# Moving dispatch operations, a dummy matmul and fourteen relus in a recurrent kernel with routed experts

## What is computed

```python
def step(carry, inp):
    h_ssm = silu(h_ssm @ A.T + bxt)
    y_ssm = h_ssm @ Cw.T + Cb + dxt
    hh = h_rnn @ W_hh.T + b_hh
    r = sigmoid(i_r + h_r)
    z = sigmoid(i_z + h_z)
    n = tanh(i_n + r * h_n)
    h_rnn = (1.0 - z) * n + z * h_rnn
    y_rnn = h_rnn @ proj_w.T + proj_b
    fused = gxt[:, :1] * y_ssm + gxt[:, 1:2] * y_rnn
...
h = layernorm(x) * (1 + ca) + sa
x = x + ga * attn(h)                       # 8 x 512 x 128
h = layernorm(x) * (1 + cb) + sb
x = x + gb * ffn(h)    # expert argmax(softmax(h @ gate_w.T)), relu(h @ w1[e] + b1[e]) @ w2[e] + b2[e], times its probability
```

## Time and profile before

| what | value |
|---|---|
| median of 3 runs | 695.22 us (694.72 to 696.77) |
| profiled execution, its own time | 694.69 us |
| its span | 692.8 us |
| PE busy | 673.0 us (97%) |
| DVE busy | 523.5 us (76%) |
| ACT busy | 423.8 us (61%) |
| POOL busy | 119.6 us (17%) |
| chain that ended last | PE 96%, issue 1%, DVE 1%, DMA 1% |

### The profile page before, as it was taken

How to read it: one execution, slowest core, us unless ns; L and a number is a source line. 1 busy time by engine, 2 the same in 40 slices (tenths; PEclk the granted TensorE clock), 3 DMA queues, 4 the chain that set the end, 5 groups by cost and what they waited for, 6 DMA issues and landing times.

```text
span 692.8 us, 35329 instructions
## 1 busy us (share of the span) xinstructions
PE 673.0 (97%) x13692; PEld 632.1 (91%) x13692; DVE 523.5 (76%) x3189; ACT 423.8 (61%) x2677; POOL 119.6 (17%) x211
## 2 busy tenths in 40 slices
PE   8999999999999999999999999999999999999991
PEld 5899999989999999999999999999999999998891
DVE  4777777777887777887888788888887888876463
ACT  4555555556666666567666775676667656766540
POOL 4011111111011111112112211111212212211122
PEclk9999999999999999999999999999999999999996
DMA  8916000603522100044322000552210006434262
GB/s 307 363 64 224 8 7 7 226 31 129 189 97 85 53 15 15 14 164 176 131 81 78 19 18 19 201 178 95 94 61 23 21 19 242 148 111 137 70 228 57
DMA packets 46152, 72.79 MB, mean 105 GB/s; under 512 B 6236, under 2 KB 28834, under 8 KB 45858
## 3 DMA queue, kind: packets, MB, share of 16 engines
q1 hardware_dynamic: 41922, 65.11, 26.8%
q0 software_dynamic: 2048, 4.20, 2.1%
q10 hardware_dynamic: 2016, 1.25, 0.6%
HBM read 14.44 MB, written 21.17 MB: 51 GB/s over the span
## 4 chain that ended last, share of the span: by engine, by line
PE 96%; issue 1%; DVE 1%; DMA 1%; ACT 0%; POOL 0%; POOLq 0%
PE rs_bank L1183 34%; PE nz_bank L1183 23%; PE hid_bank_b L1183 12%; PE work L1183 11%; PE y_bank L1183 9%; PE hid_bank_a L1183 7%; DMA yg<-rows,pos 0%; POOL yg L694 0%; DMA rows<-y_sb 0%; POOLq L498 0%; DVE fin_g L1168 0%; ACT hid_b L775 0%; DVE y_sb L1162 0%; DVE u L1100 0%; ACT xT L772 0%
## 5 line engine op out<-in xcount | busy, mean ns | idle before, releaser
L1183 PE MATMUL nz_bank<-h_ring,wg 128*64 128x16 f32 x4088 | 207.1, 211 | 0.0
L787 ACT ACTIVATE r_fac<-rs_bank 128x8 f32<-128x8 f32 x512 | 91.3, 178 | 170.7 <-PE rs_bank L1183 163.3
L1183 PE MATMUL rs_bank<-s_ring,ws_sb 128*64 128x128 f32 x1024 | 195.1, 272 | 0.0
L1183 PEld LDWEIGHTS nz_bank<-h_ring,wg 128*64 128x64 f32 x4088 | 160.6, 136 | 1.2
L1183 PE MATMUL rs_bank<-mw,wg 128*64 128x8 f32 x2044 | 146.4, 202 | 0.1
L1183 PE MATMUL rs_bank<-u,wg 128*64 128x8 f32 x2044 | 140.0, 206 | 0.2
L1092 DVE TENSOR_TENSOR_SCAN nz_bank<-r_fac,nz_bank 128x16 f32<-128x16 f32 x512 | 99.2, 194 | 48.4 <-ACT r_fac L787 30.8
L1183 PEld LDWEIGHTS rs_bank<-s_ring,ws_sb 128*64 128x64 f32 x1024 | 127.2, 136 | 9.3
L1096 DVE SCALAR_TENSOR_TENSOR mw<-v_fac,h_ring 128x8 f32<-128x8 f32 x512 | 85.7, 167 | 57.6
L1183 PEld LDWEIGHTS rs_bank<-mw,wg 128*64 128x64 f32 x2044 | 102.9, 135 | 19.1 <-DVE mw L1096 4.6
L793 ACT ACTIVATE v_fac<-nz_bank 128x8 f32<-128x8 f32 x512 | 90.7, 177 | 42.1
(11 more groups left out here) (162 smaller groups left out, 1077.0 us busy)
## 6 DMA issues: line engine op xcount, KB each, us to landing
wx<-w_all SPq DMA_DIRECT2D x59, 578.0 KB, 3.5
rows<-zeros SPq DMA_DIRECT2D x3, 4096.0 KB, 14.6
rows<-y_sb SPq DMA_DIRECT2D x67, 64.0 KB, 1.6
w_all<-in_w SPq DMA_DIRECT2D x2, 2048.0 KB, 15.3
xs_sb<-rows SPq DMA_DIRECT2D x55, 64.0 KB, 3.3
x_sb<-in_x SPq DMA_DIRECT2D x1, 1920.0 KB, 8.0
out<-o_sb SPq DMA_DIRECT2D x19, 64.0 KB, 2.5
out<-o_sb ACTq DMA_DIRECT2D x13, 64.0 KB, 2.0
```

Of the source, the lines that this page charges most:

```text
L787: nc.scalar.activation(r_fac[:, k, :, 1], r_cols(q, t), ACT.Tanh, scale=0.5).then_inc(rn_ready, 1)
L1183: last = nc.tensor.matmul(out[c:c + COLS], weights[:, c:c + COLS], moving, start=start, stop=stop, skip_group_check=skip_group_check)
```

## The change

There are four edits.

1. For the first four groups the ten dispatch operations no longer stand in steps 2 to 11, one in each, but in steps 6, 6, 9, 10, 10, 10, 11, 11, 12, 12. `rows_at`, from which SP's loads are written, is one step later.
2. In step 9 of a tile the dummy product of a step with room stands ahead of the transpose of h2 and not behind it.
3. The entry for step 9 is gone from `DVE_EARLY`. The units of every step stay the same; seven second relus (tiles 8, 9, 13, 15, 16, 20, 22, step 9) are ACT's where they were DVE's.
4. In the tail a second relu goes to ACT only before step (NT+1)*T = 528; seven relus of slots 51 to 54 are DVE's where they were ACT's.

```diff
-DVE_EARLY = {2: 15, 4: 15, 9: 23, 10: 23}
+DVE_EARLY = {2: 15, 4: 15, 10: 23}
...
+LAY_OUT = (6, 6, 9, 10, 10, 10, 11, 11, 12, 12)
+
+
 def dispatch_at(k, n):
 
     at = (last_tile(k) + 2) * T
-    return at + (2 + n if at < NT * T else 12 + n // 2)
+    return at + (LAY_OUT[n] if at < NT * T else 12 + n // 2)
...
-            if k < NG - 1 and what[0] in "AC" and what[2]:
+            if k < NG - 1 and u < (NT + 1) * T and what[0] in "AC" and what[2]:
                 on_act.add(what)
...
                     unit(kind, n, second)
-                if w == 9:
-                    tile_work(c, q, w, g)
                 if exists(c):
                     room = 0 if g in RELU_OPEN else ROOM - taken(g) - len(units)
                     if room == 2:
                         hold_clock(g, len(units), 2 * P)
                     if room == 1:
                         hold_clock(g, len(units), P)
+                if w == 9:
+                    tile_work(c, q, w, g)
+                if exists(c):
                     if g == 0:
```

## The result

| | before | changed |
|---|---|---|
| median | 694.97 us (693.74 to 696.77, 6 runs) | 698.24 us (698.02 to 699.07, 6 runs) |
| ratio | | 1.0047, 95% interval 1.0031 to 1.0064 |
| profiled execution, its span | 694.69, 692.8 | 698.25, 696.3 |
| last h_ring write of the recurrence | 632.48 us | 636.21 us |
| from there to the end of the span | 60.28 us | 60.11 us |

The changed kernel is slower by 3.3 us, and the place is the recurrence: its last step ends 3.73 us later, while the tail is 0.17 shorter. The page shows how little a mean can tell here. Its busy shares are those of before to within a point (PE 97%, DVE 75%, ACT 61%), and the granted clock is 0.992 again. Only the chain of waits has moved: PE has 93% of it instead of 96%, VectorE and ScalarE one point more each.

A forecast was written before the change was run, and what follows sets the result against it. Each step is bounded by a loop through three engines with 0.57 us free before the scan. Move +3.35, loads +0.25, dummy -0.5, relus +0.1, tail -0.15 give +3.05 on 695.22: 698.2 us, range 696.8 to 699.8.

The forecast's parts named there:

- What sets the end: Every recurrence step: work before the scan is free up to 0.57 us after h_ring; any excess lengthens the step equally.
- step 10, four tiles: Tiles 7, 14, 21, 28: passed, expert_f, ended in a chain make the scan 0.57 us late, 2.28 in all.
- step 11: Same four tiles: first_f then block_f make the scan 0.29 us late, 1.16 in all.
- step 12: Same four tiles: place then expert behind onehot, scan 0.12 us late, 0.48 in all, 1.1 at the upper end.
- step 6: Same four tiles: over then n_slots, scan 0.14 us late in tiles 7 and 14, 0.33 in 21 and 28; 0.94.
- removed, steps 2 to 7: Dispatch operations leaving their old steps, such as ended from step 7, give back about 1.5 us.
- The loads: SP's first-slot loads come 1.27 us later against their use; tile 21's group waits, +0.25 us (0 to 1.1).
- Rival B: First rows land late in all four groups: +1.1 us in place of +0.25, 699.1 to 702 us; chance 0.09.
- The dummy: Dummy ahead of h2's transpose: ten steps of 1.25 to 1.28 us after step 9 fall to 1.21, -0.5 us.
- rival C: Long single steps in tiles 6, 4 and 28 vanish, some 1.05 us; 693.7 with A; chance 0.04 including the unseen.
- The relus and the tail: Seven step-9 relus moved to ScalarE cost +0.1 us; seven tail relus moved to VectorE free xT copies, -0.15 us.
- Rival A: Dependent dispatch operations cost no more than independent ones, so the move nets 0.1 us: 694.8 us; chance 0.15.

The follow-up runs named there:

- the last two layouts: Dispatch steps chosen for each group, with edits 2 and 4 and fewer waits: 695.38 us; the same with a first slot's rows loaded before its weights: 693.26 us.
- the kernel with fewer waits: Changed kernel in which ended waits only for passed and expert only for expert_f: 698.74 us, 1.0027 of the kernel before.
- the first four kernels of the experiments' table: Only the new layout 700.70 us; changed without the new layout 696.16; changed with fewer waits 698.74; a layout for each group 695.38.
- the last three: Changed with all ten dispatch operations in step 10: 710.48 us; per-group layout with rows loaded before weights: 693.26; changed kernel again: 698.57.

## Why the prediction was right

The forecast was 698.2 us; the measured median is 698.24. It was right by its mechanism. That the two agree to 0.04 is luck: the forecast stood on a median of 695.22 for the kernel before, which is 694.97 with six runs. The change was put at +3.05 and measured at +3.27, with 2.2 to 4.4 as its interval, and the terms of the sum that came out too small or on the wrong group nearly cancelled against single steps.

**What sets the end.** The claim that lateness of the scan over 0.57 goes one to one into the step held in every tile to 0.02 (scans at +1.16, +0.87, +0.77, +0.92; steps of 1.77, 1.50, 1.40, 1.54).

**The move.**

| term, us | predicted | in the trace |
|---|---|---|
| step 10, four tiles | 2.28 | 2.31 |
| step 11 | 1.16 | 1.22 |
| step 12 | 0.48 | 0.79 |
| step 6 | 0.94 | 0.94 |
| removed, steps 2 to 7 | -1.5 | -1.54 |
| net | +3.35 | +3.72 |

Step 12 was mis-sized, and it is the choice that the prediction marked as one without a row. A free operation behind onehot starts 0.14 after its start (163.40 to 163.54), not the lower bound of 0.08, and four times the resulting 0.20 in place of 0.12 is the missing 0.3. The upper bound beside it was also summed wrong: with onehot's whole 0.23 and a handover ahead of place the scan comes at +0.94, which is 1.5 for four and not 1.1. Steps 10 and 6 came out within 0.02 of each term of their chains.

**The loads.** That the loads come 1.27 us later against their use held: the slack of tile 7's group fell from 2.65 to 1.37, that of tile 28's from 1.26 to 0.04. But the term of +0.25 stood on the wrong group. The prediction took tile 21's slack of 1.0 with the 4.0 us that its transfer took before. After, it landed 2.7 us after its issue, and X had 1.0 us to spare. That was no accident of one trace: tile 21's rows land 4.0 to 4.6 us after their issue in the three traces of kernels with the ten operations in steps 2 to 11, and 2.7 to 2.9 in the four with the changed kernel's layout. Why is open. Tile 28's group, "just not" by the prediction, is the one without slack. Tile view of xs_sb after, for tile 21's and for tile 28's group:

```profile
L603 SPq DMA_DIRECT2D xs_sb<-rows x2: 367/368/368, 439.8 to 442.6; - x2
...
DMA to landing us min/median/max: 2.6/2.7/2.7
```

```profile
L1186 PE MATMUL hid_bank_a<-const_sb,xs_sb x4: 272/298/323, 580.6 to 580.8; 128*64 128x128 f32 x4
L603 SPq DMA_DIRECT2D xs_sb<-rows x2: 362/365/368, 576.8 to 579.6; - x2
...
DMA to landing us min/median/max: 2.5/3.1/3.8
```

There the rows land 3.8 us after their issue at 576.8, at the moment at which they are read (580.61). It cost 0.02 us in this trace and 0.96 in the repeated run: the same code, with a landing 4.7 instead of 3.8 us after the issue. The term is thus 0 to 1 us from one execution to the next, as its bounds had it, but nothing in the one trace of before could say for which group. Rival B, all four groups late, did not come.

**The dummy.** Predicted -0.5. The ten steps fell by 0.62 in all: 0.04 each in six tiles, 0.06 to 0.07 in tiles 14, 21 and 28, and 0.20 in tile 4, where the step of 1.40 of rival C was a late h2 and went with it. PE's timeline around step 8 of tile 7, to which the earlier trace rows answers:

```profile
157.92 0.42 PE L1186 MATMUL hid_bank_b<-w_sb,const_sb 128*64 128x128 f32 x4
158.17 0.39 PE L1186 MATMUL work<-const_sb,h_ring 128*64 128x128 f32 x4
```

**The relus and the tail.** The step-9 relus cost 0.02 in five of the seven steps and 0.01 or less in two, 0.11 together, as said. In the tail the xT copy starts earlier, and the tail is 0.17 shorter (predicted 0.15). PE and ACT in the tail after, slot 53, to which the earlier trace rows answers:

```profile
649.51 0.39 PE L1186 MATMUL rs_bank<-const_sb,xs_sb 128*64 128x128 f32 x4
...
649.95 0.27 ACT L775 COPY xT<-rs_bank 128x128 f32<-128x128 f32 x1
```

The copy starts 0.44 after its product started, where it was 0.48. The gain isn't certain to reach the end. In the kernel with all but the layout the tail took 60.3 us: the three copies start earlier there too, but another transpose early in the tail stands 0.17 later. All four other kernels that have edit 4 also took 60.3 us; only the changed kernel itself, in both its traces, has the shorter tail.

**Single steps, rival C.** It expected three to vanish. Two did, those of tile 28 (0.49) and of tile 4; the one of 1.60 in tile 6 grew to 1.87, and three more appeared, in tiles 9, 24 and 30 (0.59 together). The first two did not go by chance: the repeated kernel before has both again, 1.69 and 1.40. The prediction called the one in tile 28 a late gather, and the rows speak against that. DVE's timeline of the kernel before, then the stretch ahead of it (columns as in the table above):

```profile
558.41 0.35 DVE L1168 SCALAR_TENSOR_TENSOR fin_g<-yg,prob,mod 128x128 f32<-128x128 f32 x1 [0.24 <-issue]
```

```profile
554.50:558.70 4.20, 4.20 (x92) 4.03 (x88) 3.26 (x21) 2.55 (x19) 0.00 (x0) 1.00 0.00 0
```

`fin_g` reads the gathered rows, but the DMA engines had started no transfer for 3.9 us when it began, and the 0.24 of idle time ahead of it stand right behind `over`, the first dispatch operation. In four traces (the kernel before twice, and the last two layouts) `over` stands in step 2 of tile 28 and the step takes 1.69 to 1.70; in the five without it there the step takes 1.20 to 1.21. The kernel with all but the layout has `over` there too, and takes 0.16 more in that step and 0.17 in the next. So the 0.49 belongs to what edit 1 removed, the net of the move is 3.72 - 0.49 = 3.23 against 3.35 predicted, and what the 0.24 is stays open.

So the trace after has 3.72 for the move, -0.62 for the dummy, -0.49 and +0.86 for the single steps, in all 3.47 of the measured 3.73; the remaining 0.26 is spread thinly over the other steps, 0.1 of it in those of the relus. Of the steps that grew, tile 9's is a late h2 ahead of a y_sb addition. In tile 30 h2 is later still, at +0.47 ahead of such an addition, and in tile 24 nothing follows it; those two are not explained, nor is tile 6's.

**Rival A** would have given 694.8. It was given 0.15, and it is settled by the rows of the kernel with fewer waits: two waits a group that no data needs make 1.55 us of the long steps.

## What to carry to other kernels

Where a short loop runs through several engines, find how late its next instruction may start, and cost every edit by whether the work in front of it ends by then, step by step; the busy shares won't tell. A chain of small dependent operations costs its handovers (here 0.10 us each) if it stands together and none if each link has a step of its own. A link alone is free only where its step has room: before, `ended` alone made step 7 longer by 0.20. So spread the chain, and wait only for what is read. If a small transfer that is needed first is queued behind a large one, look at its slack in every place: here the move used up all 1.26 us of one, and loading the small one first took the wait out of the trace.

## What the runs showed of the hardware that was not expected

- Behind an operation on 104 elements, the same VectorE operation (ended) starts 0.18 us after its start without a wait on it, and 0.37 with one. The handover was 0.10 to 0.11 in every one of the chains seen, behind operations of 0.16 to 0.28 us.
- PE idle for 2.21 us in one step of 3.86 was followed by 10.2 us at the lower level of its clock. The same step in tiles 14, 21 and 28 was followed by 6.8, 6.8 and 3.4 us of it. Together that cost about as much as the idle steps. Steps of 1.79 us, with PE busy for most of it, were not followed by it.
- POOL's operation on one element a partition takes 0.19 or 0.34 us, without a change to POOL's program. The longer time goes with the chip more than with the kernel: 24 to 27 executions of 64 in the first four kernels of the experiments' table, which ran on one chip, and 7 to 10 in the last three and the repeated kernel before, which ran on another; 6 and 14 in the first pair of profiles. The kernel before was not profiled on the first of these chips. What decides it stays open.
